# Columns of the feed-forward input by VectorE squares and SBUF to SBUF transfers in place of TensorE transposes

## The chip, the cores and the metric

The kernel runs on one core of a Trainium2 chip. The metric is the device time of one execution, in microseconds; less is better. The kernel before took 1339.2 us, the median of three runs (1337.36 to 1342.41).

## The reference

x is 16 batches of 128 rows of 1024 float32 numbers. Two blocks follow each other; each adds tanh(gate) times its result to x.

```
x = x + tanh(g_xattn) * cross_attention(layernorm(x), ctx, ctx)
x = x + tanh(g_ffn)   * feed_forward(layernorm(x))

feed_forward(y):                       # y seen in groups of 512 rows, 4 batches each
    base   = y @ W_org.T
    q      = mean(y over the rows of a batch) @ Wq.T
    coeffs = softmax(q @ lora_keys.T / sqrt(128))        # 8 experts
    h      = y @ lora_down[e]                            # rank 64 for each expert
    return base + sum over e of coeffs[e] * h[e] @ lora_up[e]
```

layernorm takes mean and variance over the 1024 columns and has no weights. Only the feed-forward block is touched by the change.

## The kernel before, in words

**Products.** TensorE contracts over partitions. Each float32 operand is split in a high and a low part of type fp32r, and `three_products` (line 155) makes high x high, low x high and high x low for every chunk of 128: lines 160, 161 and 162. So the feed-forward input y, which lies with rows on partitions, is needed with its 1024 columns on partitions, in eight chunks of 128x128 per batch, as `yT_hi` and `yT_lo`.

**The line of jobs.** The feed-forward stage is one list of jobs (`Line`, `Job`). Job n owns PSUM bank n modulo 8. TensorE, ScalarE and VectorE each go through the list in its order: TensorE fills the bank, ScalarE writes the high part, VectorE the low part, and then VectorE raises `emptied`. TensorE begins job n only when job n - 8 is emptied, and when the jobs that it `reads` are. A job without a TensorE part still counts as one bank in the ring. `act_pre` and `dve_pre` of a job are run by ScalarE and VectorE ahead of its own part. A job that is given these for another batch's normalisation is called the carrier.

**The groups.** There are four groups of four batches. A group has four h jobs (line 160 to 162 from `dn`; 24 matmuls each) and for each batch two output jobs of 36 matmuls (eight chunks of base, four of experts), one for each half of 512 columns. Around the output jobs of group g the input of group g + 1 is prepared, one batch at a time. The order of the list, for the first group (batches are numbered by arrival; n = 4 is the first of the second group):

```
out(0,0)  out(0,1)  y4 y4  y5 y5  out(1,0)  out(1,1)  y6 y6  out(2,0)  out(2,1)  y7 y7
out(3,0)  score  out(3,1)  spread  h h h h  y8 y8  out(4,0)  out(4,1)  y9 y9  out(5,0) ...
```

`y_norm(n)` (line 1091) loads the batch's rows from x_mid into one of two tiles `yin`, and hangs the normalisation on the carrier: n = 4 on out(0,0), 5 on out(0,1), 6 on out(1,0), 7 on out(2,0), 8 on the third h job, 9 on out(4,0), and so on. `y_jobs(n)` (line 1103) makes two jobs of four TensorE transposes each (`transpose_jobs`, line 350; the transposes are line 356), whose banks are split into `yT_hi` (line 150) and `yT_lo` (line 153); VectorE also sums the rows of each column for the experts' mean (`msum`, line 365). `yT` has five places for four batches, so that the next group's batch can be written while the present group's are read.

The score job (line 1188) multiplies msum by the key weights (line 1180) and reads all four batches of the next group; the h jobs of that group read them too. The output job empties with one VectorE instruction (line 1279) that adds the product to the residual `raw_d`; SyncE stores it and loads the next residual.

**SyncE.** All of these transfers are issued by SyncE from a list `plan`, sorted by a number that is a place in the list of jobs. SyncE waits for one step's condition before it turns to the next step.

Of the kernel before, what the change touches and what calls it, by code (L numbers as in the profile page):

```python
# [6 lines left out]
F32 = mybir.dt.float32  # L7
F32R = mybir.dt.float32r
ALU = mybir.AluOpType
ACT = mybir.ActivationFunctionType  # L10
AX = mybir.AxisListType

P = 128
# [72 lines left out]
def build(nc, x, ctx_cols, g_xattn, g_ffn, wq_cols, wk, wv_cols, biases, interference, query_mix, amp, wo_rows, bo,  # L86
          w_org_rows, down_rows, lora_up, keys_cols, w_key, out):
    NB, S, D = x.shape
# [7 lines left out]
    GB = 4  # L96
    NG = NB // GB
    GT = GB * S
    HALF = 512
# [18 lines left out]
    with top:  # L118
        def sem(name):
            return top.enter_context(nc.semaphore(name))  # L120

        def sb(name, shape, dt=F32, stack=top, align=32):
            return stack.enter_context(nc.sbuf_tensor(name, shape, dt, align_bytes=align))
# [25 lines left out]
        def split_hi(hi, bank_ap, **kw):  # L149
            return nc.scalar.activation(hi, bank_ap, ACT.Copy, **kw)  # L150

        def split_lo(lo, bank_ap, hi):
            return nc.vector.tensor_tensor(lo, bank_ap, hi.bitcast(F32), ALU.subtract)  # L153
# [32 lines left out]
        with ExitStack() as overlaid:  # L186
            yin, raw_d = ([sb(f"{n}{i}", [P, D], F32, overlaid)[:] for i in range(2)] for n in ("yin", "raw_d"))
# [162 lines left out]
        def transpose_jobs(line, tile, wait, hi, lo, sums=None):  # L350

            for half in range(2):
                def pe_fn(bank, half=half):
                    for q in range(4):
                        k = 4 * half + q
                        last = nc.tensor.transpose(bank[:, q * P:(q + 1) * P], tile[:, k * P:(k + 1) * P], ident[:])  # L356
                    return last

                part = slice(4 * half, 4 * half + 4)
                flat_hi = hi[:, part, :].rearrange("p a b -> p (a b)")  # L360
                flat_lo = lo[:, part, :].rearrange("p a b -> p (a b)")

                def empty(bank, part=part, flat_hi=flat_hi, flat_lo=flat_lo):
                    if sums is not None:
                        nc.vector.tensor_reduce(sums[:, part, :], bank[:].rearrange("p (q s) -> p q s", q=4),
                                                AX.X, ALU.add)
                    return split_lo(flat_lo, bank[:], flat_hi)
                end = line.add(Job(pe_fn, empty, act=lambda bank, flat_hi=flat_hi: split_hi(flat_hi, bank[:]),
                                   pe_wait=wait))
            return end  # L370
# [75 lines left out]
        def new_line(tag, banks=banks):  # L446
            return Line(banks, sem(f"s_filled_{tag}"), sem(f"s_scaled_{tag}"), sem(f"s_emptied_{tag}"))

        attend = top.enter_context(ExitStack())
        block = attend.enter_context(nc.Block())  # L450
        with proj, ExitStack() as st:
# [7 lines left out]
            norm = LayerNorm("x", st)  # L459
# [5 lines left out]
            line, plan = new_line("a"), []  # L465
# [24 lines left out]
            t_end, v_end, k_end = {}, {}, {}  # L490
# [108 lines left out]
            def k_job(g, c):  # L599
                last = t_end[g * GB + GB - 1]  # L600
                return projection_job(wk_end[c], last - 1, last if c == 0 else 0, *key_place(g),
                                      bias_mixed[:, 0, c:c + 1], k_rows, c, g, 2)

            def q_job(g, c):
                last = t_end[CTX + g * GB + GB - 1]
                first = (g, c) == (0, 0)
                return projection_job(wq_end[KC - 1], last - first, last if first else 0, *x_place(g), bias_mixed[:, 1, c:c + 1],
                                      q_rows, c, g, 1)
# [102 lines left out]
            for c in range(KC):  # L711
                job = k_job(0, c)
# [139 lines left out]
            for g in range(NG):  # L852
                if g == NG - 1:
                    plan.append((len(line.jobs) + 0.9, lambda sp, end=len(line.jobs): load_attention_rows(sp, end)))
                for c in range(KC if g + 1 < NG else KC - LATE):
                    if g == NG - 1 and c:
                        wo_chunk(c - 1, products_of[c - 1])
                    job = q_job(g, c)
# [53 lines left out]
        first_y = yin + [h_tiles[0], raw_d[0]]  # L912
# [3 lines left out]
        s_fstat, s_froot, s_fdone = (sem(f"s_first_{n}") for n in ("stat", "root", "done"))  # L916
# [22 lines left out]
        FIRST_ORDER = (2, 0, 1, 3)  # L939
        s_raw_d = [sem(f"s_raw_d{i}") for i in range(2)]  # L940
        with ExitStack() as st:
# [9 lines left out]
            part = [sb(f"part{i}", [P, 2, 4, 4], F32, st) for i in range(NS)]  # L951
# [30 lines left out]
            OCTS, HALVES = NB * NOCT, 2 * NB  # L982
# [55 lines left out]
            norm = LayerNorm("y", attend)  # L1038
            msum = sb("msum", [P, KC, GB], F32, attend)
# [8 lines left out]
            yT_hi = sb("yT_hi", [P, GB + 1, KC, P], F32R, attend, align=LINE)  # L1048
            spare += arriving("spare_lo", 1, GB * D)
            yT_lo = sb("yT_lo", [P, GB + 1, KC, P], F32R, attend)  # L1050
# [6 lines left out]
            s_arrive = [s_raw_d[1]] + [sem(f"s_arrive{i}") for i in range(1, len(arrive))]  # L1057
            s_up = [sem(f"s_up{i}") for i in range(LC)]
            s_yin = [sem(f"s_yin{i}") for i in range(2)]
            s_xres = [sem(f"s_xres{i}") for i in range(2)]  # L1060
            s_ost = [sem(f"s_ost{i}") for i in range(2)]
            s_small, s_smalle = sem("s_small"), sem("s_smalle")
            line, plan = new_line("d", one_bank + two_bank + v_bank + o_bank), []
# [19 lines left out]
            t_end = {}  # L1083

            ARRIVAL = [g * GB + i for g in range(NG) for i in ((0, 1, 2, 3) if g % 2 == 0 else (3, 0, 1, 2))]
            OUT_ORDER = [g * GB + i for g in range(NG) for i in ((1, 2, 3, 0) if g % 2 == 0 else (0, 1, 2, 3))]

            def slot_of(b):
                return b % GB + b // GB % 2

            def y_norm(n, job):

                b, slot, use = ARRIVAL[n], n % 2, (n - GB) // 2
                free = t_end[ARRIVAL[n - 2 if use else n - GB]]

                def load(sp):
                    line.wait_filled(sp, free)
                    sp.dma_start(yin[slot], x_mid[b * P:(b + 1) * P, :]).then_inc(s_yin[slot], 16)
                plan.append((free - 0.45, load))
                job.dve_pre = norm.vector_steps(n - GB, yin[slot], lambda dve: dve.wait_ge(s_yin[slot], 16 * (use + 1)))  # L1100
                job.act_pre = norm.scalar_step(n - GB)

            def y_jobs(n):
                b = ARRIVAL[n]
                at = slot_of(b)
                if n < GB:
                    def wait(pe):
                        pe.wait_ge(s_fdone, FIRST_ORDER.index(n) + 1)
                        if n == 2:
                            pe.wait_ge(s_max, OCTS)  # L1110
                        if n == 0:
                            pe.wait_ge(s_exp, 2 * OCTS)
                        if n == 1:
                            pe.wait_ge(s_o, HALVES)
                    tile, sums = first_y[n], msum[:, :, b:b + 1] if n < GB - 1 else None
                else:
                    tile, wait, sums = yin[n % 2], norm.done(n - GB), msum[:, :, b % GB:b % GB + 1]
                t_end[b] = transpose_jobs(line, tile, wait, yT_hi[:, at, :, :], yT_lo[:, at, :, :], sums=sums)

            def first_scores():  # L1120
# [86 lines left out]
            def spread_job(score_end):  # L1207

                flat = coefw[:].rearrange("b e r -> b (e r)")

                def spread_pe(bank):
                    for c in range(LC):
                        last = nc.tensor.matmul(bank[:, c * GB:(c + 1) * GB], flat[:, c * P:(c + 1) * P],
                                                ident[0:GB, 0:GB], start=True, stop=True)
                    return last
                return line.add(Job(spread_pe, lambda bank: nc.vector.tensor_copy(coefc[:].rearrange("p c b -> p (c b)"),
                                                                                  bank[:, 0:LC * GB]), reads=score_end))
# [99 lines left out]
            for n in FIRST_ORDER[:3]:  # L1317
                y_jobs(n)
# [26 lines left out]
            for g in range(NG):  # L1345
                if g:
                    for c in range(LC):
                        h_end = h_job(g, c, coef_end)
                    carrier = line.jobs[-2]
                for i in range(GB):  # L1350
                    n, more = g * GB + i, g + 1 < NG
                    if more and n:

                        y_norm(n + GB, carrier)
                        y_jobs(n + GB)
                    carrier = out_job(n, 0, h_end)
                    if more and i == GB - 1:
                        score_end = score_job(g + 1)
                    if n == 0:
                        y_norm(GB, carrier)  # L1360
                        carrier = out_job(n, 1, h_end)
                        y_jobs(GB)
                        continue
                    out_job(n, 1, h_end)
                    if more and i == GB - 1:
                        coef_end = spread_job(score_end)
# [480 lines left out]
```

## Time and profile before

| | us |
|---|---|
| median of three runs | 1339.2 |
| the profiled execution | 1343.88 |
| its span | 1342.1 |
| TensorE busy | 1323.2 |
| VectorE busy | 703.3 |
| GpSimd busy | 567.5 |
| ScalarE busy | 409.6 |

The profile is of one execution. PE is TensorE, PEld its weight loads, DVE is VectorE, ACT is ScalarE, POOL is GpSimd, SP is SyncE; a trailing q (SPq) is a queue's issue of a transfer. The feed-forward groups run from about 990 us to the end of the span. L with a number is a line of the kernel. "idle before" is the time in which the engine had nothing to do ahead of an instruction, and the arrow names what ended it.

### The profile page before, as it was taken

Reading aid. Unit: us, or ns where it says so; the run is one execution under the profiler, and the core shown is the slowest. Engines: PE = TensorE matmul, PEld = TensorE weight load, DVE = VectorE, ACT = ScalarE, POOL = GpSimd, SP = SyncE. Lnnn points to the kernel's source line nnn. Section 1 sums busy time; section 2 is a strip of 40 time slices with the busy share of each in tenths; the row PEclk is TensorE's granted clock in tenths of the full one; section 3 lists DMA queues with packets and bytes.
Section 4 is the critical chain, followed back from the end, with each engine's and each line's share of the span. In section 5 each row is a group of like instructions: output and inputs, shape, how many; then the busy total and the mean of one; then the engine's idle time right before and its main releaser. Section 6 shows DMA issues by size and latency. Waiting matters only on the chain.

```text
span 1342.1 us, 22259 instructions
## 1 busy us (share of the span) xinstructions
PE 1323.2 (99%) x8352; PEld 1113.5 (83%) x8352; DVE 703.3 (52%) x1371; ACT 409.6 (31%) x743; POOL 567.5 (42%) x777
## 2 busy tenths in 40 slices
PE   8999999999999999999999999999999999999999
PEld 7888887888888888787888888888788888888887
DVE  5333334435855545576777777777966144253110
ACT  3322221111222222355655555555451120111100
POOL 1799999999800000455566565655600000000000
PEclk9999999999999999999999999999999999999999
DMA  6898736434446677998987887777542202211011
GB/s 227 254 308 222 202 95 202 158 142 157 157 140 178 165 185 187 283 258 239 235 232 228 237 234 221 222 219 221 180 181 110 79 16 94 79 63 63 32 41 54
DMA packets 188940, 228.17 MB, mean 170 GB/s; under 512 B 26529, under 2 KB 124961, under 8 KB 188833
## 3 DMA queue, kind: packets, MB, share of 16 engines
q1 hardware_dynamic: 162096, 188.07, 47.0%
q10 hardware_dynamic: 26736, 38.68, 9.9%
q8 instruction: 67, 1.10, 0.3%
q14 instruction: 41, 0.33, 0.1%
HBM read 141.74 MB, written 83.89 MB: 168 GB/s over the span
## 4 chain that ended last, share of the span: by engine, by line
PE 83%; POOL 12%; DMA 2%; issue 1%; SPq 1%; ACT 1%; DVE 1%; ACTq 0%; POOLq 0%; DVEq 0%
PE bank L160 17%; PE bank L162 17%; PE bank L161 17%; PE bank L1471 5%; POOL mixed_part L792 5%; PE bank L1491 4%; PE bank L1506 4%; PE bank L1452 4%; PE bank L1453 4%; PE bank L1454 4%; POOL mixed_sum L799 3%; PE bank L356 2%; POOL mixed_sum L792 2%; POOL value_in L799 2%; PE bank L1478 1%
## 5 line engine op out<-in xcount | busy, mean ns | idle before, releaser
L1659 DVE TRANSPOSE_TENSOR_REDUCE part<-bank 128x16 f32<-128x512 f32 x256 | 174.1, 692 | 3.7 <-PE bank L1471 1.3
L1605 ACT ACTIVATE probT<-bank 128x512 f32<-128x512 f32 x256 | 139.0, 595 | 93.4 <-PE bank L1491 90.0
L1452 PE MATMUL bank<-w_hi,oT_hi 128*128 128x512 f32 x256 | 108.8, 425 | 0.9 <-POOL oT_lo L1772 0.5
L1279 DVE SCALAR_TENSOR_TENSOR raw_d<-bank,gates,raw_d 128x512 f32<-128x512 f32 x32 | 24.0, 750 | 163.0 <-PE bank L162 163.0
L582 DVE SCALAR_TENSOR_TENSOR stage_lo<-bank,bias_mixed,stage_hi 128x512 fp32r<-128x512 f32 x46 | 34.4, 750 | 128.8 <-ACT stage_hi L584 128.8
L160 PE MATMUL bank<-place_a,w_hi 128*128 128x512 f32 x256 | 100.4, 392 | 1.0 <-DVE place_a L153 1.0
L1453 PE MATMUL bank<-w_lo,oT_hi 128*128 128x512 f32 x256 | 101.2, 395 | 0.0
L1454 PE MATMUL bank<-w_hi,oT_lo 128*128 128x512 f32 x256 | 101.0, 395 | 0.0
L160 PE MATMUL bank<-place_b,place_a 128*128 128x512 f32 x256 | 100.0, 391 | 0.9 <-DVE place_c L153 0.9
L160 PE MATMUL bank<-w_hi,yT_hi 128*128 128x512 f32 x256 | 100.9, 394 | 0.0
L161 PE MATMUL bank<-w_lo,yT_hi 128*128 128x512 f32 x256 | 99.7, 389 | 0.0
L162 PE MATMUL bank<-w_hi,yT_lo 128*128 128x512 f32 x256 | 99.7, 389 | 0.0
L162 PE MATMUL bank<-place_a,w_lo 128*128 128x512 f32 x256 | 99.6, 389 | 0.0
L161 PE MATMUL bank<-place_a,w_hi 128*128 128x512 f32 x256 | 99.6, 389 | 0.0
L161 PE MATMUL bank<-place_c,place_a 128*128 128x512 f32 x256 | 99.6, 389 | 0.0
L162 PE MATMUL bank<-place_b,place_a 128*128 128x512 f32 x256 | 99.6, 389 | 0.0
L1700 DVE TENSOR_REDUCE negmax<-bank 32x32 f32<-32x128 f32 x128 | 35.7, 279 | 103.5 <-PE bank L1478 103.5
L799 POOL TENSOR_TENSOR mixed_sum<-mixed_sum,mixed_part 128x512 f32<-128x512 f32 x64 | 86.2, 1346 | 5.0
L160 PE MATMUL bank<-place_b,w_hi 128*128 128x512 f32 x216 | 85.4, 395 | 0.0
L1757 POOL CAST neg<-negmax 32x32 fp32r<-32x32 f32 x128 | 26.0, 203 | 138.5 <-DVE negmax L1700 90.1
L161 PE MATMUL bank<-place_b,w_hi 128*128 128x512 f32 x216 | 84.4, 391 | 0.0
L162 PE MATMUL bank<-place_b,w_lo 128*128 128x512 f32 x216 | 84.3, 390 | 0.0
(241 smaller groups left out, 3078.5 us busy)
## 6 DMA issues: line engine op xcount, KB each, us to landing
k_rows<-stage_hi SPq DMA_DIRECT2D x128, 128.0 KB, 2.8
v_pad<-v_out SPq DMA_DIRECT2D x32, 512.0 KB, 2.6
v_place<-v_pad ACTq DMA_DIRECT2D x64, 256.0 KB, 4.1
tin<-in_ctx_cols SPq DMA_DIRECT2D x26, 512.0 KB, 4.2
k_in<-k_rows SPq DMA_DIRECT2D x64, 192.0 KB, 3.0
q_in<-q_rows SPq DMA_DIRECT2D x128, 96.0 KB, 3.3
q_rows<-wq_own SPq DMA_DIRECT2D x81, 128.0 KB, 2.5
raw_d<-x_mid SPq DMA_DIRECT2D x17, 512.0 KB, 3.3
```

The costliest lines, as they stand in the source:

```text
L160: nc.tensor.matmul(bank_ap, sh, mh, start=(i == 0), stop=False)
L161: nc.tensor.matmul(bank_ap, sh, ml, start=False, stop=False)
L162: last = nc.tensor.matmul(bank_ap, sl, mh, start=False, stop=(i == len(chunks) - 1))
L792: last = pool.tensor_tensor(new[:, :, a, :, :, :].rearrange("p c d h x -> p c d (h x)"), old[:, :, m % 2, :, :, m // 2].unsqueeze(4).to_br ...
L799: then(pool.tensor_tensor(mixed_sum[:] if m < 3 else cols, mixed_sum[:], mixed_part[:], ALU.add))
L1452: pe.matmul(o_bank[out][:], hi[:, c, :], wo_hi[:, k, cols], start=(k == 0), stop=False)
L1453: pe.matmul(o_bank[out][:], hi[:, c, :], wo_lo[:, k, cols], start=False, stop=False)
L1454: last = pe.matmul(o_bank[out][:], lo[:, c, :], wo_hi[:, k, cols], start=False, stop=(k == KC - 1))
L1471: last = pe.matmul(dst, k_in[slot][0:ROWS, p, :], q_in[slot][0:ROWS, :, p, :], start=True, stop=True, skip_group_check=True)
L1491: last = pe.matmul(dst, k_in[slot][:, p, :], q_in[slot][:, :, p, :], start=True, stop=True, skip_group_check=True)
L1605: act.activation(probT[o % NPT][:, i].rearrange("k a p q -> k (a p q)"), two_bank[i][:], ACT.Exp).then_inc(s_exp, 1)
L1659: dve.tensor_reduce(part[o % NS][:, :, 2 * i:2 * i + 2, :].rearrange("k a p b -> k a (p b)"), one_bank[i][:].rearrange("k (a b t) -> k a b ...
```

## The change

Batches 4 to 15 are not transposed by TensorE any more. After the normalisation of a batch VectorE transposes each square of 32x32 within itself, from `yin` into a new tile `yturn` (one for all batches). SyncE then puts the squares in their places: square (i, j) of each 128x128 chunk belongs at (j, i), and sixteen transfers, one for each pair, move 32 partitions x 8 chunks x 32 numbers from `yturn` back into `yin`. The two jobs of a batch have no TensorE part; ScalarE and VectorE split and sum `yin` straight from SBUF. They wait for all sixteen transfers, and ScalarE also for TensorE's end of the job ahead, whose place in `yT` is written anew. Batches 0 to 3 stay as they were.

```diff
+            s_yturn, s_ycols = sem("s_yturn"), [sem(f"s_ycols{i}") for i in range(2)]
+            yturn = sb("yturn", [P, D], F32, attend)
+            BLOCK = 32
+            SQUARES = P // BLOCK
             def y_norm(n, job):
                 b, slot, use = ARRIVAL[n], n % 2, (n - GB) // 2
                 free = t_end[ARRIVAL[n - 2 if use else n - GB]]
                 def load(sp):
-                    line.wait_filled(sp, free)
+                    if use:
+                        sp.wait_ge(line.emptied, free)
+                    else:
+                        line.wait_filled(sp, free)
                     sp.dma_start(yin[slot], x_mid[b * P:(b + 1) * P, :]).then_inc(s_yin[slot], 16)
                 plan.append((free - 0.45, load))
-                job.dve_pre = norm.vector_steps(n - GB, yin[slot], lambda dve: dve.wait_ge(s_yin[slot], 16 * (use + 1)))
+                normalise = norm.vector_steps(n - GB, yin[slot], lambda dve: dve.wait_ge(s_yin[slot], 16 * (use + 1)))
+                def turn_squares(dve):
+                    normalise(dve)
+                    dve.wait_ge(norm.s_done, n - GB + 1)
+                    if n > GB:
+                        dve.wait_ge(s_ycols[(n - 1) % 2], y_columns_in(n - 1))
+                    dve.transpose(yturn[:], yin[slot]).then_inc(s_yturn, 1)
+                def place_squares(sp):
+                    sp.wait_ge(s_yturn, n - GB + 1)
+                    by_square = yturn[:].rearrange("p (k j t) -> p j k t", j=SQUARES, t=BLOCK)
+                    columns = yin[slot].rearrange("p (k i t) -> p i k t", i=SQUARES, t=BLOCK)
+                    for i in range(SQUARES):
+                        for j in range(SQUARES):
+                            sp.dma_start(columns[j * BLOCK:(j + 1) * BLOCK, i],
+                                         by_square[i * BLOCK:(i + 1) * BLOCK, j]).then_inc(s_ycols[slot], 16)
+                job.dve_pre = turn_squares
                 job.act_pre = norm.scalar_step(n - GB)
+                plan.append((line.jobs.index(job) + 0.7, place_squares))
+            def column_jobs(n):
+                b, tile = ARRIVAL[n], yin[n % 2]
+                at = slot_of(b)
+                def landed(eng):
+                    eng.wait_ge(s_ycols[n % 2], y_columns_in(n))
+                def free(act):
+                    landed(act)
+                    line.wait_filled(act, len_at[n])
+                for half in range(2):
+                    cols, part = slice(half * HALF, (half + 1) * HALF), slice(4 * half, 4 * half + 4)
+                    hi, lo = (y[:, at, part, :].rearrange("p a b -> p (a b)") for y in (yT_hi, yT_lo))
+                    def empty(bank, cols=cols, part=part, hi=hi, lo=lo):
+                        nc.vector.tensor_reduce(msum[:, part, b % GB:b % GB + 1],
+                                                tile[:, cols].rearrange("p (q s) -> p q s", q=4), AX.X, ALU.add)
+                        return split_lo(lo, tile[:, cols], hi)
+                    len_at[n] = len(line.jobs)
+                    t_end[b] = line.add(Job(None, empty, act=lambda bank, cols=cols, hi=hi: split_hi(hi, tile[:, cols]),
+                                            act_wait=free, dve_wait=landed))
...
                         y_norm(n + GB, carrier)
-                        y_jobs(n + GB)
+                        column_jobs(n + GB)
...
                         y_norm(GB, carrier)
                         carrier = out_job(n, 1, h_end)
-                        y_jobs(GB)
+                        column_jobs(GB)
```

The load of a tile `yin` for its second and later use waits for the columns to be emptied, where it waited for TensorE's transposes. In `y_jobs` only the part for the first four batches is left.

## Rows read from the trace of the kernel before

**Rows 1.** The page's first part: busy us, share of span, instructions
```profile
PE 1323.2 (99%) x8352; PEld 1113.5 (83%) x8352; DVE 703.3 (52%) x1371; ACT 409.6 (31%) x743; POOL 567.5 (42%) x777
```

**Rows 2.** Busy time by stretch: length, each engine, granted clock, DMA share, GB/s
```profile
1020.00:1060.00 40.00, 40.00 (x199) 33.09 (x198) 16.12 (x38) 4.17 (x9) 0.00 (x0) 1.00 0.24 89
```

**Rows 3.** The chain that ended last, from 990 us: start, us, what
```profile
by line: PE bank L160 31.9%; PE bank L162 31.5%; PE bank L161 31.5%; PE bank L356 3.0%; PE bank L1213 0.8%; PE bank L1180 0.4%; DVE raw_d L1279 0.2%; issue 0.0%
...
1012.23 1.75 PE bank L356 x16
...
1030.32 0.87 PE bank L356 x8
...
1056.58 0.48 PE bank L1180 x16
...
1149.13 0.48 PE bank L1180 x16
...
1241.67 0.48 PE bank L1180 x16
```

**Rows 4.** The transposes, line 356: ns min/median/max, first and last start
```profile
L356 PE MATMUL bank<-ident,yin x112: 270/272/273, 957.0 to 1233.2; 128*128 128x128 f32 x112
```

**Rows 5.** Groups of VectorE from 940 us: busy, mean ns, idle before
```profile
L153 DVE TENSOR_TENSOR yT_lo<-bank,yT_hi 128x512 fp32r<-128x512 f32 x32 | 21.6, 679 | 0.0
...
L153 DVE TENSOR_TENSOR w_lo<-up_hi_first,w_hi 128x1024 fp32r<-128x1024 f32 x4 | 4.8, 1214 | 0.0
...
L1679 DVE STREAM_TRANSPOSE inv<-rec 128x512 f32<-128x512 f32 x2 | 1.4, 704 | 0.0
```

**Rows 6.** Timeline of VectorE: start, us, engine, line, operation, idle before
```profile
1005.66 0.81 DVE L406 TENSOR_SCALAR yin<-yin,ln_mv_y,ln_rstd_y 128x1024 f32<-128x1024 f32 x1
...
1007.05 0.68 DVE L394 BATCH_NORM_STATS2 ln_stats_y<-yin 128x6 f32<-128x512 f32 x1
...
1010.00 0.81 DVE L406 TENSOR_SCALAR yin<-yin,ln_mv_y,ln_rstd_y 128x1024 f32<-128x1024 f32 x1
...
1020.48 0.69 DVE L394 BATCH_NORM_STATS2 ln_stats_y<-yin 128x6 f32<-128x512 f32 x1 [2.27 <-DMA yin<-x_mid]
...
1082.76 0.81 DVE L406 TENSOR_SCALAR yin<-yin,ln_mv_y,ln_rstd_y 128x1024 f32<-128x1024 f32 x1
```

**Rows 7.** Issues by SyncE: ns min/median/max, start of first and last; DMA queue; landing
```profile
1016.01 0.91 SPq L1098 DMA_DIRECT2D yin<-x_mid  x2
...
L548 SPq DMA_DIRECT2D q_rows<-wq_own x6: 575/624/626, 407.6 to 410.9; - x6
...
DMA to landing us min/median/max: 2.5/2.5/2.5
...
402.20 9.35 SPq L548 DMA_DIRECT2D q_rows<-wq_own  x12
...
L1383 SPq DMA_DIRECT2D q_in<-neg x64: 521/527/553, 560.9 to 939.3; - x64
...
L201 SPq DMA_DIRECT2D q_in<-q_rows x128: 303/451/1944, 543.1 to 925.7; - x128
...
L1294 SPq DMA_DIRECT2D out_x<-raw_d x15: 337/338/338, 1013.0 to 1323.3; - x15
...
q1 hardware_dynamic: 162096, 188.07, 47.0%
```

**Rows 8.** TensorE around an idle stretch: timeline, then granted clock (third from last)
```profile
612.63 0.39 PE L1454 MATMUL bank<-w_hi,oT_lo 128*128 128x512 f32 x1
615.96 0.73 PE L1491 MATMUL bank<-early_q,early_k 98*128 98x256 f32 x4 [2.94 <-DMA early_q<-neg]
...
618.73 0.63 PE L1452 MATMUL bank<-w_hi,oT_hi 128*128 128x512 f32 x1
619.16 0.63 PE L1453 MATMUL bank<-w_lo,oT_hi 128*128 128x512 f32 x1
...
619.00:620.00 1.00, 1.00 (x3) 0.72 (x3) 1.00 (x2) 0.81 (x2) 0.00 (x0) 0.50 1.00 254
```

More of the change, by code:

```diff
@@ new lines, in y_norm, with y_columns_in @@
+                job.dve_pre = turn_squares
+                job.act_pre = norm.scalar_step(n - GB)
+                plan.append((line.jobs.index(job) + 0.7, place_squares))
+            def y_columns_in(n):
+                return 16 * SQUARES * SQUARES * ((n - GB) // 2 + 1)
+            def column_jobs(n):
[16 more added lines that the diff above has]
+                                            act_wait=free, dve_wait=landed))
@@ L1103, in y_jobs @@
+            len_at = {}
             def y_jobs(n):
@@ L1105, in y_jobs, with wait @@
                 at = slot_of(b)
[L1106 to L1117, printed above, removed]
+                def wait(pe):
+                    pe.wait_ge(s_fdone, FIRST_ORDER.index(n) + 1)
+                    if n == 2:
+                        pe.wait_ge(s_max, OCTS)
+                    if n == 0:
+                        pe.wait_ge(s_exp, 2 * OCTS)
+                    if n == 1:
+                        pe.wait_ge(s_o, HALVES)
+                tile, sums = first_y[n], msum[:, :, b:b + 1] if n < GB - 1 else None
                 t_end[b] = transpose_jobs(line, tile, wait, yT_hi[:, at, :, :], yT_lo[:, at, :, :], sums=sums)
```

## The prediction, made before the result was known

> **What bounds the kernel now.** I read the page's first part, then the busy time by stretch, then the chain of work that ended last, and last the timelines of VectorE and SyncE. TensorE is the bound: 1323.2 of 1342.1 us busy, while VectorE has 703.3 and ScalarE 409.6 [rows 1]. In a stretch of 40 us inside the feed-forward groups TensorE is busy for all 40, VectorE for 16.1, and the DMA engines for 0.24 of the time [rows 2]. The chain from 990 us to the end is TensorE for about 98%, and line 356, the transposes, holds 3.0% of that window (352 us), 10.5 us [rows 3]. So anything taken off TensorE there shortens the span, as long as nothing that TensorE waits for gets later.
>
> **What the change removes.** Twelve of the sixteen batches (n = 4 to 15) lose their eight TensorE transposes, 96 in all. The mean of 272 ns [rows 4] is latency, since they overlap. The chain has the price: 1.75 us for the two batches that stand together and 0.87 us for each of the ten others [rows 3], 1.75 + 10 x 0.87 = 10.45 us. That is 0.8% of the time, and it is the most that the change can bring.
>
> **What it adds for one batch.** VectorE turns the normalised rows in 32x32 squares (call its time T), SyncE waits for that and issues 16 transfers, each of 32 partitions x 8 pieces of 128 bytes, 256 pieces; then ScalarE and VectorE split from SBUF what they split from PSUM.
> - T: the same operation at 128x512 takes 0.70 us. Twice that, 1.41, is the upper bound; the element-wise operation that took 0.68 at 512 and 1.21 at 1024 columns [rows 5] has a fixed part of about 0.15, which makes 1.26. I take 1.3.
> - Split and sums: one ScalarE pass (0.6) and four VectorE passes 0.6 apart, 3.0 us from the data to "emptied". The pass from SBUF cost 1.21 us per 1024 columns [rows 5], the same 0.6 per half, so nothing changes here. Call it C.
> - The normalisation: 3.75 us from its first statistics at 1007.05 to the end of the scaling at 1010.81 [rows 6]. Call it N.
> - P, from the turn to the last square landed. No row shows such transfers. The nearest are the stores of the query rows: also issued by SyncE from SBUF, in three dimensions, 64 x 4 = 256 pieces. Their issue takes 0.62 us, six of them start from 407.6 to 410.9, one every 0.66, and they land 2.5 us after issue [rows 7]. With 15 x 0.66 = 9.9, plus 2.5, plus 0.1 for the semaphore, P = 12.5 us. The one kind of small transfer within SBUF, 64 pieces of 128 bytes to two partitions, took 0.53 us to issue [rows 7]; with a gap of 0.04 that would make 15 x 0.57 + 2.6 = 11.1. From below: a transfer of whole rows takes 0.30 to 0.34 us to issue, and 15 x 0.30 + 2.0 = 6.5. From above: twelve query stores took 9.35 us with the waits among them, 0.78 each, which makes 15 x 0.78 + 2.6 = 14.3; and if the 16 DMA engines need for each piece what they need for a mean packet, 47% x 16 x 1342.1 / 162096 = 62 ns [rows 7], the 256 pieces per engine last 15.9 us and P is 18. I take 12.5, since number of pieces, dimensions, source and issuing engine are those of the query stores.
>
> The Trainium skill speaks both ways on the last bound. "DMA: Bandwidth & Descriptors", section "Specifications", asks for 512 B or more for line rate; its section "Why small descriptors are slow (HBM only)" exempts transfers from SBUF to SBUF. By the first the engines could bind (P of 18), by the second they do not and the issue does. No row of this profile shows a dense run of 128-byte pieces.
>
> **Where it lies.** TensorE does not read the new columns until the score job of the next group, which stands right after the first output job of a group's last batch and needs the columns of all four new batches emptied. The output jobs in between use the old columns and can run ahead of VectorE by the ring of eight banks. The score matmuls stood at 1056.58, 1149.13 and 1241.67 [rows 3]. So the question is when the fourth batch's columns are emptied. The steps form one loop, because the normalisation of batch n+1 stands behind the columns of batch n in VectorE's order: N + T + P + C = 3.75 + 1.3 + 12.5 + 3.0 = 20.55 us, whereas TensorE needs two output jobs per batch, 16.3 us (from the end of the first transposes, 1012.23 + 1.75, to the next at 1030.32 [rows 3]). The lag accumulates over a group.
>
> Group 0 (batches 4 to 7). The scaling of batch 4 ends at 1006.47 [rows 6]; turned 1007.8; landed 1020.3. Batch 5's turn is in VectorE's stream ahead of batch 4's columns and waits for the one buffer of turned squares, so it ends at 1021.6 and lands at 1034.1; its columns are emptied at 1037.1. Behind the waiting turn are the second output job's emptying and both pairs of columns; no TensorE job needs these yet. SyncE issues batch 5's squares until 1032.3, then the store of the first output, waits 2.6 us for it, loads its residual, and only at 1035.7 issues the load of batch 6. That lands 4.4 us later, as in [rows 6], at 1040.1. Batch 6: turned 1045.2, landed 1057.7, emptied 1060.7. Batch 7: turned 1065.7, landed 1078.2, emptied 1081.2. The score job starts there and not at 1056.6: 24.6 us later.
> Groups 1 and 2 begin with batch 8's (12's) scaling ending at 1083.57 [rows 6], turned 1084.9, landed 1097.4, emptied 1100.4; three more loops of 20.55 end at 1162.0, against 1149.13: 12.9 us later, twice. These lags are against the old times of the score job, so the removed transposes up to each are already in them (all twelve batches lie ahead of a score job). Sum: 24.6 + 12.9 + 12.9 = 50.4 us. Every us of P moves it by 12 us while all three stalls stand.
>
> The clock. Where TensorE had stood idle from about 613 to 615.96, the granted clock then was 0.50 (1.2 GHz), still so at 619 to 620, and matmuls started 0.43 apart and not 0.23 [rows 8]: from 616.9 to 620 a loss of some 1.6 us. After each of three stalls of 16 to 28 us I expect the same: +5 us.
> The Trainium skill ("TensorE: Matmul & The Clock Gate", section "Part 1: The HAM clock gate") says that an idle array falls to 1.2 GHz. The trace agrees: 0.50 after the idle stretch.
>
> Edits at nothing: output stores and residual loads wait behind the squares on SyncE for some 10 us, but VectorE needs a residual only after the columns that are later still. The last group has no squares. ScalarE gains no work.
>
> Total: 1343.9 (the profiled execution's own time; its span is 1342.1) + 50.4 + 5 = 1399.3. The runs' median is 1339.2, 4.7 below the profiled execution, so 1395 us.
>
> **Rivals.**
> - Issue is cheap. If 16 transfers go out at 0.30 to 0.36 us, as whole-row transfers do, P is 6.5 to 7.5. Groups 1 and 2 then have no stall (the loop falls below 16.3 at a P of 8.3) and bring 3.5 us each, while group 0 stands at 24.6 - 4 x 6 = +0.6 or +4.6. Sum -6.4 to -2.4: 1333 to 1337, not slower. It decides from P of about 8.5 down. For it: half a megabyte in whole rows is issued in that time [rows 7]. Against: every store of 256 pieces took at least 0.57. To be faster by more than 0.5% the issue would have to be quicker than any row.
> - The DMA engines bind on small pieces: P = 18, 12 x 5.5 = 66 more, 1461 us. For it: the mean packet of 62 ns. Against: that mean is of packets of 188.07 MB / 162096 = 1160 bytes, nine times as long, and this stretch has the DMA engines three quarters idle [rows 2].
> - A rival in between, the pace of 0.78: P = 14.3, 1417 us; it belongs to my own case's upper end.
> - That the transposes would not leave TensorE can't be: the new jobs have no TensorE part.
>
> **Numbers.** Forecast (P of 11 to 14.3, 1377 to 1417 us) 0.70; engines bind or the pace is well above 0.8, 0.18; cheap issue 0.12. The range that holds 8 in 10 leaves out cheap issue and the far half of the dear case: 1355 to 1437. A change of 0.5% (6.7 us) is about what these runs can tell. Faster by more 0.05; within 0.05; slower 0.90 (of the cheap case a small part is still above 1346).
>
> **What would show it.** SyncE's timeline: sixteen issues per batch, 0.66 apart; if 0.35, the first rival. Landing of the last 2 to 3 us after its issue; if ever later from one to the next, the DMA engines. VectorE and ScalarE idle before the sums, on the DMA. TensorE idle three times, before the score matmuls (line of the score job), about 28, 16 and 16 us, released by VectorE's last column subtraction, and the granted clock at 0.50 for some 3 us behind each. The line of transposes with 16 matmuls from yin instead of 112. The prediction is wrong if TensorE has no idle stretch ahead of the score jobs, or if it stalls earlier, in an output job, on a bank.

## The result, and the profile after

The changed kernel takes 1390.6 us, median of four runs, against 1340.1 us of the kernel before beside it: a ratio of 1.0383, 95% interval 1.0361 to 1.0404. It is 50.5 us slower; 1395 was forecast. Its profiled execution took 1391.6 us with a span of 1389.8.

The page's first part, and the stretch of 40 us that [rows 2] shows:

```profile
PE 1316.8 (95%) x8256; PEld 1106.9 (80%) x8256; DVE 715.6 (51%) x1383; ACT 410.1 (30%) x743; POOL 567.7 (41%) x777
```
```profile
1020.00:1060.00 40.00, 28.69 (x126) 23.08 (x124) 15.19 (x33) 2.71 (x6) 0.00 (x0) 0.92 0.40 115
```

TensorE has 96 matmuls and 6 us less than in [rows 1], and is no longer busy throughout. Its waits, summed (engine, line, releaser: us in total, times, longest), show one new line that outweighs the rest:

```profile
PE bank L1232 <- DVE yT_lo L153: 55.5, 3, 25.6
PE bank L319 <- DVE place_b L153: 3.2, 1, 3.2
```

Line 1232 is the score job's matmul. It waits three times for VectorE's last column subtraction, as foreseen: 25.6, 15.4 and 14.5 us. The chain that ended last, from 990 us, answers to [rows 3]; TensorE had 98% of it before:

```profile
by line: SPq L1123 27.6%; PE bank L160 12.2%; PE bank L161 11.7%; PE bank L162 11.7%; DMA yin<-yturn 6.2%; issue 4.9%; DVE yturn L1115 3.8%; DVE yT_lo L153 3.4%; DVE yin L406 2.3%; ACT yT_hi L150 1.8%; DVE ln_stats_y L394 1.7%; DVE ln_stats
```

Line 1123 on SyncE's queue is the issue of the squares. The instructions on the turned tile (count: ns min/median/max, first and last start) give the two prices that no row of before had, and the issues of one batch in SyncE's timeline give their pace:

```profile
L1123 SPq DMA_DIRECT2D yin<-yturn x192: 585/611/1043, 1003.1 to 1282.2; - x192
L1115 DVE STREAM_TRANSPOSE yturn<-yin x12: 1245/1246/1250, 1001.9 to 1271.1; 128x1024 f32<-128x1024 f32 x12
...
DMA to landing us min/median/max: 1.9/1.9/3.6
```
```profile
1147.06 10.41 SPq L1123 DMA_DIRECT2D yin<-yturn  x16
1157.52 0.60 SPq L1346 DMA_DIRECT2D out_x<-raw_d  x1
1160.37 0.33 SPq L1341 DMA_DIRECT2D raw_d<-x_mid  x1
1161.98 0.32 SPq L1106 DMA_DIRECT2D yin<-x_mid  x1
1166.94 10.39 SPq L1123 DMA_DIRECT2D yin<-yturn  x16
```

One round of the loop, as the chain has it (start, us, what); of the sixteen issues the first and the last are shown:

```profile
1140.20 0.68 DVE yT_lo L153
...
1142.07 0.60 DVE ln_stats_y L394
...
1145.79 1.26 DVE yturn L1115
1147.05 0.02 issue
1147.06 0.59 SPq L1123
...
1156.21 0.61 SPq L1123
1156.82 0.04 issue
1156.86 1.92 DMA yin<-yturn
...
1158.81 0.64 ACT yT_hi L150
```

The reader is to see that nothing in it overlaps: turn to 1147.05, issues one every 0.65 us, the last square landed at 1158.78, then the split, the next statistics and the next turn at 1165.67. P is 11.7 us and the loop 19.9, where TensorE has 16.3.

### The profile page after: what moved, and what is told of

Read it like the earlier page. It is cut to its first block, busy times and chain, and to the rows that moved or that the text cites. A ratio compares the mean times of both kernels' runs of the same rounds, so it can differ in the third digit from the quotient of the medians.

```text
span 1389.8 us, 22306 instructions
## 1 busy us (share of the span) xinstructions
PE 1316.8 (95%) x8256; PEld 1106.9 (80%) x8256; DVE 715.6 (51%) x1383; ACT 410.1 (30%) x743; POOL 567.7 (41%) x777
## 4 chain that ended last, share of the span: by engine, by line
PE 66%; POOL 11%; SPq 8%; DVE 6%; DMA 3%; issue 2%; ACT 2%; ACTq 0%; DVEq 0%; POOLq 0%
PE bank L160 12%; PE bank L161 12%; PE bank L162 12%; SPq L1123 8%; PE bank L1523 5%; POOL mixed_part L792 5%; PE bank L1543 4%; PE bank L1558 4%; PE bank L1504 4%; PE bank L1505 4%; PE bank L1506 4%; POOL mixed_sum L799 3%; DMA yin<-yturn 2%; POOL mixed_sum L792 2%; POOL value_in L799 2%
## 5 line engine op out<-in xcount | busy, mean ns | idle before, releaser
L584 ACT ACTIVATE stage_hi<-bank,bias_mixed 128x512 fp32r<-128x512 f32 x46 | 31.5, 687 | 164.2 <-PE bank L162 139.8
```

## The experiments

Ratios are against the kernel before, run beside each of them. The changed kernel stands at 1.0383. Diffs are against the changed kernel.

### Two queues

```diff
-                def place_squares(sp):
-                    sp.wait_ge(s_yturn, n - GB + 1)
+                def place_squares(eng, rows=range(SQUARES // 2)):
+                    eng.wait_ge(s_yturn, n - GB + 1)
...
+                second_half[n] = lambda act: place_squares(act, range(SQUARES // 2, SQUARES))
...
                     t_end[b] = line.add(Job(None, empty, act=...,
-                                            act_wait=free, dve_wait=landed))
+                                            act_wait=free, dve_wait=landed,
+                                            act_pre=None if half else second_half[n]))
```

> Of the sixteen transfers of a batch SyncE issues eight and ScalarE the other eight. Theory (the issue by one engine is what takes the time: 16 starts 0.65 us apart and 1.9 us to land, 11.7 us): 8 starts and 1.9 make 6.6 to 7, the loop of a batch falls from 19.9 to about 14.8 us, under TensorE's 16.3. Groups 1 and 2 lose no time and keep their 3.5 us each; in group 0 a stall of some 6 us is left, since batch 5 still waits for the one buffer. About 1337 us (1332 to 1343). Rival (the 16 DMA engines, or one shared descriptor generator, set the pace of the small pieces): each engine's issues get twice as long or land later, the last square still lands 11 to 12 us after the turn, and the time stays at 1385 or more.

Measured: 1342.4 us, 1.0023 (1.0013 to 1.0032). 47 of the 50 us are gone, so issue by one engine (or by its queue; each of the two has its own) is the cost, and neither the DMA engines nor a shared generator of descriptors sets the pace. Both queues keep nearly the single queue's time per issue:

```profile
L1123 SPq DMA_DIRECT2D yin<-yturn x96: 585/612/1317, 1006.5 to 1235.2; - x96
L1123 ACTq DMA_DIRECT2D yin<-yturn x96: 592/638/1886, 1008.8 to 1235.6; - x96
```

It is 5 us above what was expected, and this lies in group 0, where TensorE waits 9.9 us and not some 6; groups 1 and 2 gain their 3.6 us each. The four P of group 0 are 9.0, 6.9, 8.3 and 6.9 us where 6.6 to 7 were expected. In batch 4 ScalarE's first issue (1008.8) comes 2.3 us after SyncE's (1006.5); in batch 6 single issues took up to 1.3 us and landings up to 3.1 (see also "Two queues, two buffers, an earlier load").

### More transfers, fewer pieces

```diff
-                            sp.dma_start(columns[j * BLOCK:(j + 1) * BLOCK, i],
-                                         by_square[i * BLOCK:(i + 1) * BLOCK, j]).then_inc(s_ycols[slot], 16)
+                            for k in (slice(0, KC // 2), slice(KC // 2, KC)):
+                                sp.dma_start(columns[j * BLOCK:(j + 1) * BLOCK, i, k],
+                                             by_square[i * BLOCK:(i + 1) * BLOCK, j, k]).then_inc(s_ycols[slot], 16)
...
-                return 16 * SQUARES * SQUARES * ((n - GB) // 2 + 1)
+                return 32 * SQUARES * SQUARES * ((n - GB) // 2 + 1)
```

> The same 4096 pieces of a batch go out in 32 transfers of 128 pieces instead of 16 of 256. If an issue costs per piece, one takes 0.33 us and the time is the same 1390 us. If it costs per transfer, as whole rows of 128 pieces in 0.32 to 0.44 us and 64 pieces in 0.53 us leave open, each stays near 0.6 us: the last square lands 32 x 0.65 + 2 = 22 us after the turn, 10.4 us later than now, and with twelve such steps in the chain the time is about 1515 us. Between them (0.43 us each, the back to back issue of whole rows): 13.9 + 2, some 50 us more, 1440. I hold the one between for likeliest.

Measured: 1514.3 us, 1.1307 (1.1291 to 1.1324). I held the case between the two for likeliest; it was the case in which an issue costs per transfer. In the chain an issue of 128 pieces takes 0.60 us, one of 256 took 0.61:

```profile
1149.80 0.60 SPq L1124
1150.44 0.60 SPq L1124
1151.09 0.60 SPq L1124
```

The time rose by 124 us over the changed kernel's, and 12 steps x 10.4 us were worked out: 125. That is the slope of the sum, 12 us for each us of P, measured. The stalls no longer stand only ahead of the score job: 131.0 us are there, and 39 us more in four waits ahead of output matmuls (line 160, on VectorE's `raw_d` three times and `yT_lo` once). This does not change the slope, since the chain of a group runs through the batches' loop and not through TensorE's output jobs.

### One piece of 1 KB per partition

```diff
-                    dve.transpose(yturn[:], yin[slot]).then_inc(s_yturn, 1)
+                    dve.transpose(yturn[:].rearrange("p (j k t) -> p j k t", j=SQUARES, t=BLOCK),
+                                  yin[slot].rearrange("p (k j t) -> p j k t", j=SQUARES, t=BLOCK)).then_inc(s_yturn, 1)
...
-                    by_square = yturn[:].rearrange("p (k j t) -> p j k t", j=SQUARES, t=BLOCK)
-                    columns = yin[slot].rearrange("p (k i t) -> p i k t", i=SQUARES, t=BLOCK)
+                    by_square = yturn[:].rearrange("p (j f) -> p j f", j=SQUARES)
+                    columns = yin[slot].rearrange("p (i f) -> p i f", i=SQUARES)
...
+                    src = tile.rearrange("p (i k t) -> p k i t", i=SQUARES, t=BLOCK)[:, part]
```

> Same squares, same sixteen transfers, same bytes, one engine; but VectorE writes the turned squares sorted by their target and the columns lie sorted by source, so that a transfer is 32 partitions x one piece of 1 KB (two dimensions) and not 32 x 8 pieces of 128 bytes (three). Theory as the 32-transfer run left it (an issue costs about 0.6 us by its form, whatever the number of pieces): with two dimensions it falls to the 0.32 to 0.44 us of whole rows. P = 15 x 0.35 + 2.0 = 7.3 us, the loop 15.5 us, below TensorE's 16.3; only group 0 stalls, some 8 us: about 1340 us (1335 to 1350). Rival (each transfer costs 0.6 us, whatever its form): 1390. Rival (the drain of 128-byte pieces): also 1340, but with issues still at 0.6 us.

Measured: 1386.6 us, 1.0357 (1.0341 to 1.0373). The first rival holds (each transfer costs 0.6 us) and my theory of the form falls: behind one another, with two dimensions and an eighth of the pieces, issues still take 0.59 us. Alone the form counts a little: the first issue of a batch, some 5 us after the issue before it, took 0.51 us here and 0.59 in the changed kernel.

```profile
L1124 SPq DMA_DIRECT2D yin<-yturn x192: 507/591/1184, 1002.2 to 1275.3; - x192
...
DMA to landing us min/median/max: 1.7/1.8/2.8
```

The 0.02 us less per issue and 0.1 in landing, 0.4 us of P, would be 5 us; 3.5 are there. If the DMA engines' drain of 128-byte pieces has a part in the stall, it is no more than the 0.1 us of landing in each P.

### Two buffers of turned squares

```diff
+                yturn = yturns[slot]
...
-                    if n > GB:
-                        dve.wait_ge(s_ycols[(n - 1) % 2], y_columns_in(n - 1))
+                    if use:
+                        dve.wait_ge(s_ycols[slot], y_columns_in(n - 2))
```

> A second buffer of turned squares, so that batch 5 is turned without waiting 8 us for batch 4's squares to land. Theory (SyncE's issue is the chain): its 32 issues follow one another at once, so only the landing (1.9), the turn (1.25) and a hop leave the chain of group 0, 3.3 us, and nothing in the others: 1387 us. Rival (the one buffer is what costs, 8 us of wait): 1382 or less.

Measured: 1388.8 us, 1.0372 (1.0358 to 1.0385). The rival's 1382 (1.031) is outside; the gain itself, some 1.5 us by the ratios, is within their intervals. VectorE's wait of 8.0 us is gone from the profile, yet the score job of group 0 stands only 2.1 us closer to batch 4's scaling (71.0 us and not 73.1; the longest wait is 24.5 us and not 25.6). Most of the wait ran beside SyncE's issues. Of the 3.3 us expected 0.9 went to a single issue that took 1.48 us (1003.40).

### Two queues, two buffers, an earlier load

```diff
-                plan.append((free - 0.45, load))
+                plan.append((free - 0.45 - (1.0 if n == GB + 2 else 0), load))
```

and both edits above.

> Squares issued by both SyncE and ScalarE, two buffers of turned squares, and the load of batch 6 ahead of the first output's store. Group 0: batch 5's squares land about 3 us earlier than with two queues alone and batch 6 is loaded 4 us earlier, which leaves a stall of 0 to 3 us ahead of the first score job. Groups 1 and 2 have none. All but some 2 us of the 10.45 us of transposes are gained: about 1332 us (1329 to 1336), faster than before. If the DMA engines bind, above 1380.

Measured: 1339.5 us, 1.0007 (0.9996 to 1.0019): no difference from before where 1332 was expected. Groups 1 and 2 gain what they should, 3.57 us each: their spread jobs (line 1268) stand 88.97 us apart, before they stood 92.54 apart. Group 0 does not:

```profile
1019.43 0.33 SPq L1107 DMA_DIRECT2D yin<-x_mid  x1
1019.81 0.55 SPq L1349 DMA_DIRECT2D out_x<-raw_d  x1
1025.14 0.33 SPq L1344 DMA_DIRECT2D raw_d<-x_mid  x1
1028.65 0.33 SPq L1107 DMA_DIRECT2D yin<-x_mid  x1
1033.62 6.10 SPq L1124 DMA_DIRECT2D yin<-yturn  x8
1039.76 0.60 SPq L1349 DMA_DIRECT2D out_x<-raw_d  x1
```
```profile
1020.95 4.50 DMA yin<-yturn
...
1037.19 1.87 ACTq L1124
1039.09 0.72 ACTq L1124
1040.14 3.60 DMA yin<-yturn
```
```profile
PE bank L1235 <- DVE yT_lo L153: 9.5, 1, 9.5
```

The first fence is SyncE's timeline, the second the chain (ScalarE's queue and the landings), the third TensorE's one wait. In group 0 a square landed 4.5 and 3.6 us after its issue and one issue took 1.87 us, where 1.9 and 0.63 are the rule. Ahead of the 4.5 (1020.95) a load of yin and an output store had just been issued, ahead of the 3.6 (1040.14) an output store; beside the slow issue (1037.19) there were only the other queue's squares, eight of which took SyncE 6.10 us and not 5.2. Other transfers are not the whole of it: in the changed kernel one square landed 3.55 us after its issue (1115.51), and SyncE had issued nothing but squares since 1091.60. Also ScalarE begins batch 4's half only behind batch 5's square root, at 1009.57, 2.3 us after SyncE. What delays a landing or an issue was not taken apart and stays open.

### The first group as before

```diff
+                if not by_squares(n):
+                    return y_jobs(n)
...
+            def by_squares(n):
+                return n >= 2 * GB
```

> Batches 4 to 7 are transposed by TensorE as before; only 8 to 15 go by squares. By the trace the stall of group 0 (25.6 us), its clock (2.9) less its gain (3.5) is 25 us of the 50: about 1366 us, with two stalls of 15 us as now. Rival (a lag carried over from one group to the next): the second group's stall gets shorter without the first's, under 1360.

Measured: 1367.9 us, 1.0208 (1.0192 to 1.0224). The two stalls left add up to 31.6 us, the longest 16.9; nothing is carried from one group to the next. Group 0's share of the loss is 1.0383 - 1.0208, 23 us.

### Only every second batch

The same edit with `n % 2 == 0`.

> Only batches 4, 6, 8, ... go by squares, the odd ones by TensorE, so that each step P of 11.7 us has two batches' time (32.6 us) instead of one. Groups 1 and 2 then have no stall and bring 1.7 us each; in group 0 TensorE waits some 5 us for batch 7's normalisation, which stands behind batch 6's columns, and brings 1.7. About 1341 us (1336 to 1346). If the squares cost by their number and not by the loop, half of the 50 us is left: 1365.

Measured: 1342.5 us, 1.0025 (1.0014 to 1.0036). With two batches' time for each P the score jobs wait no more. The one stall foreseen is there, 7 us in place of 5, ahead of batch 7's transposes:

```profile
1052.20 1.94 PE L356 MATMUL bank<-ident,yin 128*128 128x128 f32 x8 [6.98 <-DVE yin L406]
```

Its 1.94 us for eight transposes, twice the 0.87 to 1.04 of the others, is the clock: 0.50 from 1052 to 1055, behind the idle stretch.

### TensorE kept busy in the stalls

```diff
+                if job.fill:
+                    pe.wait_ge(self.emptied, n + 1 - ring)
+                    job.fill(self.bank(n))
...
+                def fill(bank):
+                    for _ in range(108 if g == 1 else 60):
+                        nc.tensor.matmul(bank[:], wg_hi[:, 0, 0:P], wg_lo[:, 0, 0:HALF], start=True, stop=True)
```

> The changed kernel with matmuls that compute nothing used (108, 60 and 60 of them) put between the first output job of a group's last batch and the wait of the score job, into the score job's own bank. They fill 24.5 and 13.6 us of the stalls of 25.6 and 15. Theory (the stretches at 1.2 GHz behind the stalls cost 2.9 + 2.3 + 2.3 us): the granted clock stays at 2.4 GHz and the time falls by 7 us, to 1383.5. Rival (the clock costs nothing, as the chain runs through SyncE): 1390.

Measured: 1386.9 us, 1.0353 (1.0338 to 1.0368). The changed kernel ran with the clock at 0.50 behind a stall; the last three numbers of a row are granted clock, DMA share and GB/s:

```profile
1049.00:1074.00 25.00, 0.28 (x2) 0.00 (x0) 9.82 (x20) 3.63 (x6) 0.00 (x0) 0.59 0.39 110
1075.00:1080.00 5.00, 5.00 (x27) 3.99 (x26) 1.64 (x6) 0.30 (x2) 0.00 (x0) 0.50 0.56 192
1081.00:1086.00 5.00, 5.00 (x24) 4.01 (x22) 0.00 (x0) 0.00 (x0) 0.00 (x0) 1.00 0.00 0
```

With the fillers the same stretch has

```profile
1047.00:1075.00 28.00, 26.82 (x119) 21.88 (x117) 9.80 (x20) 3.62 (x6) 0.00 (x0) 1.00 0.38 103
```

and the span's mean is 1.00. From the score matmul to the spread job's the changed kernel needs 11.33, 10.77 and 10.93 us, this one 8.87: 6.4 us in three. The runs show 4 us by the ratios where 7 were expected, and the intervals of the two overlap slightly. So the price of the slow stretches is shown in the profile; in the time it points the same way, and its size there is not settled.

### Two queues, and the first two batches by TensorE

The two-queue edit, with `by_squares(n)` as `n >= GB + 2`.

> Squares issued by SyncE and ScalarE, eight transfers each, and only for batches 6 to 15; 4 and 5, whose squares must follow one another at once, are transposed by TensorE as before. With two queues the second and third group already gained 3.57 us each (spread job to spread job 88.97 and not 92.54 us), and the first lost 9.5 to 9.9 us in one stall. Here batch 6's squares start some 8 us earlier against TensorE, so that no score job waits: ten batches of 0.87 us gained, 8.7 us, 1331 us (1329 to 1334), faster than both kernels. If group 0 still stalls (transfers of both queues beside the loads of yin and the residuals landed up to 4.6 us after issue), 1334 to 1340.

Measured: 1330.7 us, 0.9925 (0.9906 to 0.9944), faster than both kernels: 10 us less than the one before, where 8.7 were worked out. TensorE's wait ahead of the score job is gone (last output matmul, then line 1248):

```profile
1048.55 0.39 PE L162 MATMUL bank<-up_hi,h_lo 128*128 128x512 f32 x1
1048.87 0.55 PE L1248 MATMUL bank<-key_w,msum 128*4 128x8 f32 x16
```

## Why the prediction was right

Step by step, against its own terms, in the profiled executions:

| step | predicted | measured |
|---|---|---|
| turn (T) | 1.3 | 1.25 |
| normalisation (N) | 3.75 | 3.7 |
| landed to the next statistics (C) | 3.0 | 3.2 |
| pace of issue, landing, P | 0.66, 2.5, 12.5 | 0.65, 1.9, 11.7 |
| the loop | 20.55 | 19.9 |
| score job later, group 0 | 24.6 | 23.0 |
| score job later, groups 1 and 2 | 12.9 twice | 11.9 and 10.9 |
| clock after the stalls | 5 | 6.4 |
| sum | 55.4 | 52.2 |

The lags are taken from the end of the first batch's scaling to the score matmul: 1001.81 to 1074.90 and 1104.42 to 1181.84, against 1006.47 to 1056.58 and 1083.57 to 1149.13 [rows 3, 6]. The span grew by less, 47.7 us, because the changed kernel's execution reached that first scaling 4.7 us earlier; nothing of the change is ahead of it, and where the execution before stood idle for 2.94 us and then ran at the slow clock [rows 8], this one waited for such a transfer 0.7 us at the longest. The forecast came down by as much, 4.7 us, from the profiled execution to the median; that the two are one difference is not shown.

**Right, and shown.** The transposes' worth: groups without a stall keep 3.57 us of four batches, 4 x 0.87 and a little. The bound: 47 us go with a second issuing queue. The place: three waits ahead of the score matmul. The one wait in an output job, on a bank that VectorE had not emptied, is 0.59 us (1040.81), and the stall of 25.6 us behind it swallows it; by the letter it touches a sign that was to refute the prediction, by its size it does not. The slope: 124 us for 10.4 us more of P. The clock: three stretches at 0.50.

**Right for a reason that fell.** That the pace of 0.66 came out at 0.65 is in part luck. I took the query stores' 0.66 us because they have 256 pieces and three dimensions. Behind one another neither counts for more than 0.02 us: 128 pieces cost 0.60 and 32 pieces in two dimensions 0.59. The row that was nearest in kind was the other one that I read, the small transfers within SBUF at 0.53 [rows 7]; by it P was 11.1, and the measured 11.7 lies between the two. What does set the 0.6 stays open. An output store of whole rows took 0.60 directly behind the squares and 0.34 by itself, so part of that store's time comes of what is issued ahead of it. For the squares this can't be the whole: the first of a batch, with no issue for some 5 us ahead of it, took 0.59 already, and 0.51 as one piece per partition.

**Mis-sized.** The landing (1.9, not 2.5: it was read from stores to HBM), worth 0.6 x 12 = 7 us too much; and the clock, 6.4 and not 5. In the stretch that I read, the clock fell only after TensorE had resumed at 615.96 (it was 0.85 in the mean from 616 to 617); behind the first stall it was at 0.50 from the first matmul at 1074.90 and stayed so until about 1080.6, for 5.7 us and not for some 3. Part of the first error was made good by others. The twelve P add up to 143.3 us and not to 150, since four lasted 12.0 to 13.4 us with slow issues or landings in them; C was 0.2 us longer ten times, and batch 6's load came 0.7 us later. Together that is 4.0 of the 4.6 us by which the three lags fell short. The first rival (cheap issue) failed on its premise of 0.30 to 0.36. Its price for group 0, +0.6 to +4.6 us, held the four P to be all 6.5 to 7.5. With the P of the two-queue run (31.1 us for the four) the same working gives 24.6 - 18.9 = 5.7, and 6.4 were measured there. The second (the DMA engines at 62 ns a piece) failed too.

On "DMA: Bandwidth & Descriptors" of the Trainium skill: its exemption of transfers within SBUF from the penalty on small pieces (section "Why small descriptors are slow (HBM only)") agrees with these runs, since pieces of 1 KB in place of 128 bytes moved the landing only from 1.9 to 1.8 us. The same page's section "Issuing engines are not separate DMA queues" says that issuing on several engines only saves the sequencer's time to initiate, which is usually small beside the transfer itself. Here an issue is 0.61 us beside 1.9 to the landing, but sixteen stand in a row, and that saving was 47 of 50 us.

## What to carry to other kernels

Count the issues of a step, not its bytes: sixteen small transfers by one engine are 10 us in a row, and they bind as soon as they stand in a loop with the next batch's work. Moving work off the busiest engine pays only if the path that replaces it, with all its waits in series, is shorter than that engine's time per round; where it is longer, give the issues two queues or every second round. Where a group starts with two rounds back to back, the new path has no slack there, and the old way may stay for just these.

## What was not expected of the hardware

- Issued behind one another, transfers within SBUF took 0.59 to 0.61 us each to issue, for 32, 128 and 256 pieces alike; alone, 0.51 for 32 pieces and 0.59 for 128 and 256.
- Two queues issued side by side at 0.61 and 0.64 us each, with single issues up to 1.9 us; landings reached 4.6 us, some with a transfer of half a megabyte just issued. With one queue, one square landed 3.6 us after its issue with no such transfer near it.
- After the first stall, of 25.6 us, TensorE worked 5.7 us at a granted clock of 0.50; after the second and third, of 15.4 and 14.5 us, some 4.6 and 5.
